# A fused decoder layer on one core: sums one slot earlier, the keys' low half moved ahead, four bias adds moved to POOL

## What is computed

```python
x = x + _L0_attn_ref(_layernorm(x, axis=-1), ...)
# with, inside:
c_q = h_t @ W_DQ + b_DQ
c_kv = h_t @ W_DKV + b_DKV
...
scores = jnp.einsum('bhsd,bhtd->bhst', q, k) * scale
attn = jax.nn.softmax(scores, axis=-1)
o = jnp.einsum('bhst,bhtd->bhsd', attn, v_c)
o = o.transpose(0, 2, 1, 3).reshape(b, s, N_HEADS * D_K)
return o @ W_O + b_O
# then the router of the next layer:
logits = jnp.einsum('bsd,de->bse', context, Wg) + bg
scores_topk, idx_topk = jax.lax.top_k(logits, K)
```

## Time and profile before

| | us |
|---|---|
| median of three runs | 731.56 (730.13 to 733.31) |
| the profiled execution | 733.41 |
| its span, first to last instruction | 731.6 |
| score of tile 0 | 31.22 |
| first scatter | 77.92 |
| end of the last scatter | 203.3 |

### The profile page before, as it was taken

How to read it: one execution, slowest core, us unless ns; L and a number is a source line. 1 busy time by engine, 2 the same in 40 slices (tenths; PEclk the granted TensorE clock), 3 DMA queues, 4 the chain that set the end, 5 groups by cost and what they waited for, 6 DMA issues and landing times. The chain is left out here.

```text
span 731.6 us, 10978 instructions
## 1 busy us (share of the span) xinstructions
PE 651.0 (89%) x3408; PEld 457.8 (63%) x3408; DVE 548.4 (75%) x1321; ACT 347.3 (47%) x633; POOL 345.7 (47%) x400
## 2 busy tenths in 40 slices
PE   8967888786669999999982998999999999999997
PEld 8635555554657777777761755666666666666664
DVE  4777888889248999999964786877868695958564
ACT  3845577653025666666663434344343435253221
POOL 5223787777758999999956423050403122000000
PEclk9978999999889999999995999999999999999999
DMA  8900130000133566676211474454544545353442
GB/s 215 381 27 1 46 93 30 33 30 38 44 101 112 168 178 204 179 196 178 79 58 44 99 164 118 111 138 115 135 114 123 142 122 138 90 141 110 128 115 58
DMA packets 74871, 84.13 MB, mean 115 GB/s; under 512 B 15345, under 2 KB 43995, under 8 KB 74814
## 3 DMA queue, kind: packets, MB, share of 16 engines
q1 hardware_dynamic: 69688, 74.93, 37.1%
q0 software_dynamic: 4288, 8.40, 3.9%
q10 hardware_dynamic: 838, 0.11, 0.1%
HBM read 64.48 MB, written 18.87 MB: 114 GB/s over the span
## 5 line engine op out<-in xcount | busy, mean ns | idle before, releaser
L883 ACT ACTIVATE r_s<-bank 128x512 f32<-128x512 f32 x136 | 81.0, 597 | 149.6 <-PE bank L1457 136.9
L1677 PE MATMUL pair_banks<-t_s,Dn 128*128 128x512 f32 x272 | 137.9, 592 | 0.7 <-issue 0.7
L1192 DVE TENSOR_TENSOR h1l<-r,h1h 128x512 fp32r<-128x512 f32 x92 | 113.0, 1246 | 18.1 <-POOL h1h L610 18.1
L1307 DVE TENSOR_TENSOR rc_s<-r_s,score_banks 128x512 f32<-128x512 f32 x90 | 61.5, 683 | 47.9 <-ACT r_s L883 29.5
L1455 PE MATMUL bank<-fxh,Gh 128*128 128x512 f32 x136 | 95.1, 699 | 0.0
L1320 DVE TENSOR_TENSOR t_s<-rc_s,bcb 128x512 f32<-128x512 f32 x128 | 87.4, 685 | 3.7 <-DMA bcb<-c_rows 3.0
L610 POOL TENSOR_SCALAR h1h<-r 128x512 fp32r<-128x512 f32 x92 | 73.5, 803 | 21.7 <-ACT r L829 19.7
L629 POOL TENSOR_TENSOR mvp<-mvp,meps 128x4 f32<-128x4 f32 x8 | 1.6, 197 | 170.0 <-DVE mvp L1230 170.0
L549 POOL DMA_INDIRECT x_sorted<-xsb,posi x64 | 63.6, 994 | 28.3 <-DVE xsb L1106 15.3
L621 POOL DMA_INDIRECT yg<-y_sorted,posi x64 | 62.9, 983 | 24.9 <-issue 18.4
L1677 PEld LDWEIGHTS pair_banks<-t_s,Dn 128*128 128x128 f32 x272 | 51.4, 190 | 16.0 <-issue 5.0
(11 more groups left out here) (295 smaller groups left out, 1575.2 us busy)
## 6 DMA issues: line engine op xcount, KB each, us to landing
bcb<-c_rows SPq DMA_DIRECT2D x128, 256.0 KB
wraw<-in_L_xattn_W SPq DMA_DIRECT2D x46, 256.0 KB
x_sorted<-wraw SPq DMA_DIRECT2D x1, 5888.0 KB, 19.1
xg<-x_sorted SPq DMA_DIRECT2D x23, 256.0 KB, 3.5
y_sorted<-ysb SPq DMA_DIRECT2D x23, 256.0 KB, 3.0
ctxb<-in_ctx SPq DMA_DIRECT2D x8, 256.0 KB, 4.6
out<-x_all SPq DMA_DIRECT2D x8, 256.0 KB
x_all<-in_x SPq DMA_DIRECT2D x2, 512.0 KB, 6.1
```

Source lines behind the costliest of these rows:

```text
L883: act.activation(r_s[:, n % RB2, :], bank[n % 3][:, :], ACT.Silu).then_inc(F["act"], 1)
L1192: tt(h1l[:, n % NB1, :], r1[:, n % RB1, :], h1h[:, n % NB1, :].bitcast(F32), ALU.subtract)\
L1307: tt(rc_s[:, n % CB2, :], r_s[:, n % RB2, :], bank[3 + n % 3][:, :], ALU.mult).then_inc(F["rc"], 1)
L1677: mm(bank[6][:, :], Dn[:, weights_of(p), :], t_s[:, n % TB2, :], start=(p == 0), stop=(p == NC2 - 1))\
```

## The change

Seven edits, all in the attention stage or ahead of it.

1. Every lag from `sum` on is one less. On DVE the sum, the reciprocal and (from tile 29) the normalisation stand behind the slot's maximum, no longer in front of it.
2. `kvlo` goes from -3 to -4, behind the maximum of the slot before the keys. It waits for a semaphore of `kvS` alone and not for the copy behind it. For group 1 it was ahead of tile 0's maximum and is now behind it.
3. The statistics of tiles 16 to 31 are taken in slots -4 to -1, as one part.
4. The bias of groups 0 to 3 is added by POOL in its slots 4 to 7, behind the normalisation; groups 4 to 7 stay on DVE.
5. `router1_counts` goes from the head of slot 6 to the end of slot 5; the output of tile 1 stands behind the values in slot 6 and waits for it, and `ranks` waits for the first residual.
6. The last half of x is loaded ahead of W_O and the last four context loads.
7. Warm-up products whose results nobody reads: 14, 4 and 8 become 5, 2 and 3, and four stand in slot 2.

```diff
-            cq=((-5, 0),), kvS=((-4, 0),), cqS=((-3, 0),), kvlo=((-3, 0),),
+            cq=((-5, 0),), kvS=((-4, 0),), cqS=((-3, 0),), kvlo=((-4, 0),),
...
-LAG = dict(exp=1, sum=2, norm=3, pT=4, u=5, out=6, rstd=7, xs=9, scatter=9)
+LAG = dict(exp=1, sum=1, norm=2, pT=3, u=4, out=5, rstd=6, xs=8, scatter=8)
...
+PB = 4
...
-PARTS = ((0, 4), (4, 8), (8, 16), (16, 24), (24, 32))
+PARTS = ((0, 4), (4, 8), (8, 16), (16, 32))
...
-            sp.dma_start(wo_a[:, :, :], W_O.rearrange("(h k) d -> k h d", h=H)).then_inc(s_wo, 16)
...
+            load_x(2)
+            sp.dma_start(wo_a[:, :, :], W_O.rearrange("(h k) d -> k h d", h=H)).then_inc(s_wo, 16)
             for i in range(4, NS):
                 load_ctx(i)
-            load_x(2)
...
+            rstd1(3)
             for n in range(NT + TAIL):
                 m = n - LAG["norm"]
                 if 0 <= m < NV:
                     normalise_p(m)
-                if n == 1:
-                    rstd1(3)
-                if n == 7:
-                    rstd1(4)
-                    router1_positions()
+                if n == 4:
+                    pool.wait_ge(s_N, 2)
+                if 4 <= n < 4 + PB:
+                    add_out_bias(n - 4)
                 m = n - LAG["rstd"]
                 if 0 <= m < NT and m % 2 == 1:
                     rstd_pair(m)
+                if n == 7:
+                    router1_positions()
...
-                    act.activation(kvS[:, q, :], bank[2][:, :], ACT.Identity, bias=bkv[:, :])
+                    act.activation(kvS[:, q, :], bank[2][:, :], ACT.Identity, bias=bkv[:, :]).then_inc(A["kvs"], 1)
...
-                if n == -1:
-                    dve.wait_ge(s_xin[2], 16)
-                if n in (-1, 0, 5, 6):
-                    first = {-1: 16, 0: 20, 5: 24, 6: 28}[n]
-                    statistics(first, first + 4)
+                if n == -4:
+                    dve.wait_ge(s_xin[2], 16)
+                if -4 <= n <= -1:
+                    statistics(32 + 4 * n, 36 + 4 * n)
...
-                    dve.wait_ge(A["kvh"], m + 1)
+                    dve.wait_ge(A["kvs"], m + 1)
...
-            unread(bank[6], 14)
+            unread(bank[6], 5)
...
+                pe.wait_ge(A["x1"], 1)
...
-                if 0 <= n - LAG["out"] < NT:
+                if 0 <= n - LAG["out"] < NT and n != 6:
                     output(n - LAG["out"])
...
+                if n == 2:
+                    unread(bank[0], 4)
```

More of the change, by code:

```diff
@@ L319, in decoder_kernel @@
         A = {n: sem("at_" + n) for n in (
-            "xn xo xT xh xl kv_ps kvh kv cq_ps cq k_ps kst v_ps vh s_ps max sm exp sum rden p pv pT_ps ph "
+            "xn xo xT xh xl kv_ps kvs kvh kv cq_ps cq k_ps kst v_ps vh s_ps max sm exp sum rden p pv pT_ps ph "
             "u_ps uh o_ps x1 bst mva eps rstd xs").split()}
@@ L564, in router1_positions, with add_out_bias @@
                 pool.tensor_copy(posi[:, :, :], posf[:, :, :]).then_inc(s_pos, 1)
+            def add_out_bias(m):
+                pool.wait_ge(A["xn"], m + 1)
+                xr = x_all[:, m * TPS:(m + 1) * TPS, :]
+                pool.tensor_tensor(xr, xr, obb[:, :].unsqueeze(1).to_broadcast([P, TPS, D]), ALU.add).then_inc(A["xo"], 1)
+            rstd1(3)
             for n in range(NT + TAIL):
@@ L964, in statistics_rest @@
             def statistics_rest(n):
+                if n == -4:
+                    dve.wait_ge(s_xin[2], 16)
+                if -4 <= n <= -1:
+                    statistics(32 + 4 * n, 36 + 4 * n)
                 if n == -1:
[L966 to L973 removed]
+                    variance_eps(3)
+                if n == 2:
+                    negated_mean1(3)
             def context(q):
@@ L1068, in router1 @@
                     router1_picked()
+                if n == 5:
+                    router1_counts()
                 if n == 6:
@@ L1076, in add_out_bias @@
             def add_out_bias(m):
-                if m == 0:
-                    dve.wait_ge(s_N, 2)
                 dve.wait_ge(A["xn"], m + 1)
@@ L1131, in _ @@
                 o, u, m = n - LAG["out"], n - LAG["sum"], n - LAG["xs"]
-                if n == 6:
-                    router1_counts()
                 if 0 <= o < NT:
                     residual1(o)
-                if n == 0:
-                    head("kvlo", 1, 0)
-                for name, j, part in head_steps(n, ("kvlo",)):
-                    if j != 1:
-                        head(name, j, part)
-                if 0 <= u < NT:
-                    summed(u)
                 if 0 <= m < NT:
@@ L1147, in _ @@
                     dve.bn_stats(st6a[:, o % 2, :], x_all[:, o, :]).then_inc(A["bst"], 1)
-                if 0 <= u < NT:
-                    dve.wait_ge(A["sum"], u + 1)
-                    dve.reciprocal(rden[:, u % NP, :, :], ssum[:, u % NP, :, :]).then_inc(A["rden"], 1)
-                    if u >= NV:
-                        dve.wait_ge(A["rden"], u + 1)
-                        at = sm[:, u % NP, :].rearrange("p (h t) -> p h t", h=H)
-                        tt(at, at, rden[:, u % NP, :, :].to_broadcast([P, H, S]), ALU.mult).then_inc(A["pv"], 1)
                 if 0 <= o < NT:
@@ L1163, in _ @@
                     maximum(n)
-                for step in head_steps(n, ("xl",)):
+                for step in head_steps(n, ("xl", "kvlo")):
                     head(*step)
+                if 0 <= u < NT:
+                    summed(u)
+                if 0 <= u < NT:
+                    dve.wait_ge(A["sum"], u + 1)
+                    dve.reciprocal(rden[:, u % NP, :, :], ssum[:, u % NP, :, :]).then_inc(A["rden"], 1)
+                    if u >= NV:
+                        dve.wait_ge(A["rden"], u + 1)
+                        at = sm[:, u % NP, :].rearrange("p (h t) -> p h t", h=H)
+                        tt(at, at, rden[:, u % NP, :, :].to_broadcast([P, H, S]), ALU.mult).then_inc(A["pv"], 1)
                 if n in CTX["copy"]:
@@ L1169, in _ @@
                 router1(n)
-                if n % TPS == 0 and 4 <= n < NT + 4:
+                if n % TPS == 0 and PB <= (n - 4) // TPS < NS:
                     add_out_bias((n - 4) // TPS)
@@ L1370, in _ @@
                 ins.then_inc(s_hps, 1)
-            unread(bank[6], 4)
+            unread(bank[6], 2)
             pe.wait_ge(s_hqk, 2)
@@ L1385, in _ @@
             ins.then_inc(s_gps, 1)
-            unread(bank[6], 8)
+            unread(bank[6], 3)
             def spread_rows():
@@ L1485, in head @@
                         pe.wait_ge(A["kv"], m + 1)
+                        pe.wait_ge(A["kvh"], m + 1)
                         if m == 0:
@@ L1505, in output @@
             def output(n):
-                if n == 0:
+                if n == 1:
                     pe.wait_ge(s_cnt, 1)
-                else:
+                if n >= 1:
                     pe.wait_ge(A["x1"], n)
@@ L1572, in _ @@
                     values(n - LAG["u"])
+                if n == 6:
+                    output(n - LAG["out"])
                 if 0 <= n < NT:
```

4 lines of the change are left out of this document (removed).

## The result

The changed kernel takes 738.46 us in the median (734.74 to 743.09), the kernel before 731.56 (730.13 to 734.72), 13 runs each. The ratio is 1.008, with a 95% interval of 1.0062 to 1.0098. The forecast was 729.3, from 725.0 to 734.5. The profiled execution took 737.3 us for a span of 735.5.

The account below looks back on a forecast made before the run. POOL, which never rests between the normalisations of tiles 24 and 28, was taken as the bound: time is the scatters' end plus a constant. Terms -2.8 + 0.5 + 0 = -2.3 us took 731.56 to 729.3, range 725.0 to 734.5.

Parts of the forecast that it names:

- Keys' low half: Once in four slots: keys' products start 0.8 us earlier, offset by a new collision; +0.5 us over five groups, bounds -4.1 and +4.5.
- the stop: DVE's scaling meets POOL's normalisation by construction, taking 1.07 us instead of 0.34; that slot's maximum starts 0.9 later.
- slower: Rival: scaling's stall reaches the path in one more slot per group, up to 0.9 us each; +3.7, 735.3 us; chance 0.12.
- The hand-overs, -2.8: Lags behind the exponential one slot shorter: tile 24 normalised at 153.7 instead of 156.44; -2.8 us, bounds 0 and -4.4.
- Router and head: Head: tile 0's score about 2 us later; router's slots: bases at 67.3, positions at 68.7 against 68.79; term 0, ends -2 and +2.
- The bias on POOL: Four adds leave DVE (0.68 us each) for POOL (about 1.05 each), three where POOL waits, the fourth ahead of the router's positions.
- the warm-up: Head: warm-up products shrink from 26 to 10; the first projection waits for DVE's low half, not for them: nothing.

Follow-up runs that it names:

- a_split: Changed kernel with PE's two key-projection products that need only xn's high half put ahead of the wait for the low half: ratio 1.0074 to the kernel before.
- a_fill: Changed kernel with six unread products on PE behind the values of each slot from 28 to 35: ratio 1.0103 to the kernel before.
- a_stats_first: Changed kernel with DVE's scaling (xsb) moved behind the slot's statistics instead of ahead of them: ratio 1.0003 to the kernel before.
- a_order_old: Changed kernel with its new lags on PE, ACT and POOL but DVE's order of before (sum at lag 2): ratio 0.9995 to the kernel before.
- b_kvlo: Kernel before with the second edit alone, the keys' low half at slot -4 behind the maximum: ratio 1.0062 to the kernel before.

## Why the prediction was wrong

**Keys' low half and the stop: the step that failed.** The mechanism was right, down to its size (a scaling near 1.0 us forecast, 0.9 in the mean). Its places were not. The prediction said that "In the slots of tiles 1 and 2 of a group DVE waits for the score longer than this stall, so it costs nothing". It set +0.1 for a group from 0.8 gained and 0.9 lost; measured were 0.88 gained, 1.09 lost ahead of the next group's first maximum, and 0.66 lost ahead of tile 2's, +0.87. Five groups at that rate cost 4.4 us, where the sum had 0.5. (Of its 0.9, give 1.07 less 0.34, 0.73; the rest had no row.) The wait there is 0.94 us in the kernel before and would have covered 0.9, but once in a group the stop was not 1.07 us as in the earlier trace rows but 1.65, since the scaling started 0.5 us ahead of the normalisation and was held all the same. The earlier trace rows show only the short form; the trace of before has a scaling of 1.84 us at 171.78, which I passed over. This is the place that the rival "slower" named; its 735.3 lies nearest to the result and had a chance of 0.12. Its 4.5 us for five groups stand beside the 4.4 above; it had taken them from the 0.9 of the short form.

**The clock.** The prediction had no term for it. Of the four groups from tile 12 on, the changed kernel lost 0.89, 0.87, 2.71 and 1.12 us against before; the 2.71 are the group with the fall at tile 22, and 1.5 of them its slot. What falls cost in the median stays open: in the profile of `a_split` this one is gone (18.38 us instead of 19.97), but the next group takes 19.22 instead of 18.37. That falls come at other places in equal code is seen in the profile of `a_fill`: with nothing changed up to slot 27 it fell behind tiles 10, 18, 22 and 24, in the changed kernel behind 22 and 24. The changed kernel's runs spread over 8.4 us, those of before over 4.6; that this comes from the falls is argued, not shown. The head varies too: with the same code up to slot 0, tile 0's score stands at 32.23 us in the profile of `a_stats_first` and at 35.26 in that of `a_fill`.

**The hand-overs, -2.8.** The rows behind it add up to 153.7 against 156.44, so 2.7. The size was right and the place wrong. Tile 24's maximum to its normalisation takes 8.5 us (151.40 to 159.86) where it took 12.0 (144.40 to 156.44), a lead of 3.6; but DVE was 7.0 late by then, so the normalisation came 3.4 us later, not 2.8 earlier. The lead appears at the end: from tile 31's maximum to its residual 14.7 us (182.12 to 196.81) instead of 17.05 (174.85 to 191.90).

**The sum, as measured.** Tile 31's maximum is 7.3 us late: 0.7 by tile 8's maximum, 1.8 in the group from there, 5.6 in the next four, less 0.85 in the last three slots. The 1.8 lie where the clock was low in both profiles (75 to 80 us: 0.66 before, 0.51 after), and how much of them the stop made is not shown. The shorter hand-overs return 2.4; the residual and the last scatter (207.28 against 202.33) are 4.9 late, and the span 3.9. The median moved by 6.9: the profiled execution of the changed kernel is 1.2 us under its median, that of before 1.85 over.

**Router and head.** Within their bounds, though each is one execution and the head's scatter above is as large: first context copy 20.78 (21.1 forecast), tile 0's score 32.33 (33.2), positions at 69.89 (68.7), tile 8's maximum at 73.53 against 72.80, first scatter 76.30 against 77.92. The bias on POOL and the warm-up cost nothing that the runs could show, as put.

**The page.** The Trainium skill ("SBUF — State Buffer", section "SBUF: two separate sides") lets whichever operation starts first keep the shared pair. Of the 20 held scalings of the changed kernel six agree clearly, their rows beginning behind the normalisation's, and in nine the two begin within 0.01 us of each other. In five the scaling's row begins some 0.5 us ahead (138.76 against 139.26) and it lost all the same. The measurement decides. What held it between is open: an indirect DMA of POOL ran then, but beside one alone scalings took 0.34 to 0.60 us in the profiles here.

## To carry to other kernels

Where one engine's small operation can be stopped by another engine's large one, take its longest form, and set it against each slot's own wait; an average slot hides that one of four has none. Put such operations in front of the instruction that releases the large one, and early enough for the in-order queue behind them. A change that shortens hand-overs can turn a chance meeting into a nearly certain one, because the other engine now waits for the release.

## What was new of the hardware

The scaling, the add of EPS and the bias add, all from SBUF to SBUF, were held until POOL's normalisation ended. This holds even for two elements in each partition (the add of EPS, 0.17 alone and 1.52 us in `a_order_old`) and even where their row starts ahead of it: by 0.58 us for the bias add of `b_kvlo` (2.20 instead of 0.68) and by 0.70 for a scaling of the kernel before (1.84 instead of 0.34, at 171.78). The sum over the exponentials (0.67 to 0.69 us), the statistics (0.28 to 0.30) and the residual, which reads PSUM (0.25 to 0.29), kept their times beside it. In the reverse case, in the changed kernel, POOL's normalisation took 1.37 us instead of 1.05 where the bias add of 0.64 us came first (134.50 and 134.67).
